# A four-batch transformer block: x of batches 2 and 3 turned into tokens by transposes, its mean taken off where the tokens are scaled

## The chip, the cores and the metric

The kernel runs on one core of a Trainium2 chip, in float32. The metric is the time of one execution in device microseconds; a kernel's time is the median of several runs. The engines are named as the profile names them: PE (TensorE), DVE (VectorE), ACT (ScalarE), POOL (GpSimd) and SP (SyncE, which only issues DMAs here).

## The reference, cut to what matters

```python
# x: (4, 96, 56, 56)
x = x + conv_attention(_ln_c(x))     # _ln_c: layer norm over the 96 channels, eps 1e-6
t = tokens(x)                        # (4, 3136, 96)
t = t + experts(_ln_t(t))            # 4 experts of width 384, the 2 best weighted by a softmax
...
def conv_attention(x):
    value = dwconv3x3(x); query = dwconv3x3(x)
    key = dwconv3x3(x, stride=2); off = dwconv3x3(x, stride=2)
    pos = tanh(offsets(gelu(norm(off))) + ref)       # (28, 28) positions
    v = bilinear_sample(value, pos)
    out = (query^T key * scale) v                    # per head, 12 heads
    return w_out @ out
```

The change concerns `_ln_c` of batches 2 and 3: `(x - mean) / sqrt(var + eps)`, with mean and variance over the channels of each pixel.

## The kernel before, in words

The five engines each run one list of instructions, written out by hand, and meet at semaphores. The four batches go through the same stages. The expert part of a batch is cut into 84 chunks of 448 tokens x 128 hidden units: three matmuls (L762 to L764), a Gelu on ACT (L1006) and a second product (L746). These chunks fill PE while DVE works on the convolutions of the next batch. How many chunks PE has issued, and how many Gelus ACT has done, before each step of the other work is given by the tables `CHUNKS_AHEAD` (PE) and `GELUS_AHEAD` (ACT), by step and position; chunk numbers run through all batches. The last 84 chunks are done alone at the end, with more exact second products.

In `rest(b)` for batch b (1 to 3) the order around the change is, on each engine:

- PE: values to tokens (L621), then `x_to_tokens(b + 1)`: x of the next batch, channels on partitions, is turned into tokens in 7 slots of 4 pieces of 112 pixels (L529), two slots between chunks; then keys (L566), chunks, then `quarters_back(b + 1)`, the "pad" blocks: 6 blocks, 3 of the upper and 3 of the lower rows, which turn the normed tokens back into channels with a halo row (L534, L551, L556). Then `key_values` (L632), `mixes`, `attended` (L662, L650).
- ACT: empties each slot of tokens into `xT` (L839), each pad block into `xpad` (L858); in `scaled` it multiplies the tokens of tiles 6, 5 and 4 by `rstd` (L831, four activations to a tile, each on 96 channels).
- DVE: `norm_x`: `bn_stats` of the tokens (L1082), `statistics` (L1059 to L1072, on 112 x 28 numbers, with three Newton steps for `rstd`), then `scale_x`, which multiplies tiles 0 to 3 by `rstd` (L1098), then `sample` (L1335, L1338).

The matmul of L529 has the matrix `ident_gate` = I - 1/96 as its moving operand, so the tokens come out with the mean already off:

```python
last = nc.tensor.matmul(bank[0:TP, j * C:(j + 1) * C], x_of(b)[:, t0:t0 + TP], ident_gate[:, 0:C], start=True, stop=True)
```

A float32 matmul stands in the trace as two records (two passes), a transpose as one. DVE signals `x_stats` when `rstd` is done; ACT's `scaled` waits for it, and the pads wait for `x_normed` (DVE's tiles) and `x_normed_act` (ACT's). PE and ACT share two PSUM banks, `pa0` and `pa1`, for the slots, the pads and some more: block n may be written when block n - 2 has been emptied. In batches 2 and 3 the tables have PE begin the pads after 69 and 145 chunks, and ACT scale its tiles at `xn=(67, 69, 69)` and `xn=(143, 144, 145)` Gelus.

POOL gathers the sampled values by indirect DMA (L1469) and adds the experts' outputs to x (L1480); DVE forms these outputs (`ye`, L1416) at points of its own list.

Of the kernel before, what the change touches and what calls it, by code (L numbers as in the profile page):

```python
# [18 lines left out]
BATCH, C, H, W = 4, 96, 56, 56  # L19
# [5 lines left out]
QUARTERS = HC // CH_PER_HEAD  # L25
QPIX = PIX // QUARTERS
SCALE = HC ** -0.5
EXPERTS, HID = 4, 4 * C
LN1_EPS, OFF_EPS, LN2_EPS = 1e-6, 1e-5, 1e-5

TP = 112
# [59 lines left out]
def dve_jobs():  # L91

    order = jobs(0, "offs", 1)
    for b in range(BATCH):
        order += jobs(b, "kv", QUARTERS) + jobs(b, "y", NY) + jobs(b, "x1c", NG)
        if b + 1 < BATCH:
# [35 lines left out]

GELUS_AHEAD = [
    dict(x1n=(0, 0, 0), x1c=(0, 0, 0, 0, 3, 3, 4), exp=(0,), gateT=(3,), offT=(10, 10), offc=(16, 17), tanh=(19,)),
    dict(valT=(42, 42, 43, 43, 44, 44, 45), xT=(45, 46, 46, 47, 47, 48, 48), keyT=(49, 49), xn=(67, 69, 69),
         pad=(69, 70, 70, 71, 71, 72), mix=(73, 73, 74, 74), x1T=(74, 74, 74, 74, 74, 74, 75), offT=(75, 76),
         x1n=(78, 80, 82), x1c=(80, 81, 83, 84, 86, 86, 87), exp=(81,), gateT=(86,), offc=(93, 94), tanh=(95,)),
    dict(valT=(118, 118, 119, 119, 120, 120, 121), xT=(121, 122, 122, 123, 123, 124, 124), keyT=(125, 125),
         xn=(143, 144, 145), pad=(145, 146, 146, 147, 147, 148), mix=(151, 151, 152, 152),
         x1T=(152, 152, 152, 152, 152, 152, 153), offT=(153, 154), x1n=(156, 158, 160),  # L140
         x1c=(158, 159, 161, 162, 164, 164, 165), exp=(159,), gateT=(164,), offc=(172, 173), tanh=(175,)),
    dict(valT=(198, 198, 199, 199, 200, 200, 201), keyT=(204, 204), mix=(233, 233, 234, 234),
# [45 lines left out]
def build(nc, t, out):  # L188
# [4 lines left out]
    with ExitStack() as ctx:  # L193
# [302 lines left out]
        def _(pe):  # L496
# [17 lines left out]
            def x_to_tokens(b, before=lambda g: None, slots=range(QT)):  # L514

                for s in slots:
                    before(s)
                    if s == 0:
                        pe.wait_ge(centred, 1)
                        if not first(b):  # L520
                            pe.wait_ge(x_in[b], 16)
                    if first(b):
                        for n, (start, end) in enumerate(X_PARTS):
                            if s == start:
                                pe.wait_ge(x_part[n], 16)
                    bank = act_bank(b, "xT", s)
                    for j in range(QUARTERS):
                        t0 = (j * QT + s) * TP
                        last = nc.tensor.matmul(bank[0:TP, j * C:(j + 1) * C], x_of(b)[:, t0:t0 + TP], ident_gate[:, 0:C], start=True, stop=True)  # L529
                    last.then_inc(act_full, 1)  # L530

            def halo(bank, at, pieces, rows):
# [3 lines left out]
            def quarters_back(b, before=lambda g: None):  # L536

                for g in range(2 * BLOCKS):
                    before(g)
                    i, low = g % BLOCKS, g // BLOCKS  # L540
                    if g == 0:
                        pe.wait_ge(x_normed, 2 * b + 1)
                        pe.wait_ge(x_normed_act, 3 * b + 1)
                    elif g == BLOCKS:
                        pe.wait_ge(x_normed, 2 * b + 2)
                        pe.wait_ge(x_normed_act, 3 * b + 3)
                    bank = act_bank(b, "pad", g)
                    if low:
                        for k in range(TOP_TILES, QT):
                            at = (k - TOP_TILES) * TP  # L550
                            nc.tensor.transpose(bank[:, at:at + TP], stationary(tiles_of(k), i), ident[0:TP, 0:TP])  # L551
                        halo(bank, LOW_PIX - W, stationary(first_tiles[:, :, 1:, :], i), 0).then_inc(act_full, 1)
                    else:
                        halo(bank, 0, stationary(last_tiles[:, :, 0:QUARTERS, :], i), 1)
                        for k in range(TOP_TILES):
                            last = nc.tensor.transpose(bank[:, W + k * TP:W + (k + 1) * TP], stationary(tiles_of(k), i), ident[0:TP, 0:TP])  # L556
                        last.then_inc(act_full, 1)
# [260 lines left out]
        def _(act):  # L818
# [22 lines left out]

            def scaled(b, before=lambda n: None):

                for n, s in enumerate(reversed(range(TOP_TILES + 1, QT))):
                    before(n)
                    act.wait_ge(x_stats, b + 1)
                    scale(x_stats_of(b), [(s * QUARTERS + j, tiles_of(s)[:, :, j, :]) for j in range(QUARTERS)]).then_inc(x_normed_act, 1)

            def padded(b, before=lambda g: None):
                for g in range(2 * BLOCKS):  # L850
# [178 lines left out]
        def _(dve):  # L1029
# [52 lines left out]
                    last = v.bn_stats(m.st[0:TP, k, :], tile(k))  # L1082
                return last

            def norm_tokens(m, b, last, eps, stats, turn):

                link(last)
                statistics(m, TP, NT, eps, False, turn).then_inc(stats, 1)
                dve.wait_ge(stats, b + 1)

            def bn_x(b, g):
                return bn(x_stats_of(b), b, g, lambda n: tiles_of(n // QUARTERS)[:, :, n % QUARTERS, :], "xT")

            def scale_x(b):
                by = x_stats_of(b).rstd[0:TP, :].rearrange("p (s o j u) -> p s o j u", j=QUARTERS, o=1, u=1)
                for s in range(TOP_TILES + 1):
                    part = tiles_of(s)
                    ins = v.tensor_tensor(part, part, by[:, s, :, :, :].to_broadcast([TP, BLOCKS, QUARTERS, CB]), ALU.mult)  # L1098
                    if s >= TOP_TILES - 1:
                        ins.then_inc(x_normed, 1)  # L1100

            def norm_x(b, turn):

                for g in range(NG):
                    last = bn_x(b, g)
                    turn()
                norm_tokens(x_stats_of(b), b, last, LN1_EPS, x_stats, turn)
                scale_x(b)
                turn()

# [427 lines left out]
```

## Time and profile before

| | |
|---|---|
| Timed runs | 748.95, 750.81, 751.0 us; median 750.81 us |
| Profiled execution, span from first to last instruction | 749.4 us |
| Busy of the span | PE 94%, PEld 66%, DVE 78%, ACT 51%, POOL 29% |
| Chain that ended last | PE 56%, DVE 19%, DMA 7%, ACT 6%, POOL 5%, issue 5% |
| Mean granted clock of TensorE | 0.985 |

The profiled execution has no time of its own in the list beside its span. Busy time is counted from the first to the last cycle of an instruction; matmuls overlap, so a busy PE can still be one that is held up. The chain is followed back from the last instruction to what released it, so it names what each stage waited for. In a timeline a row is a run of like instructions: its start, its length, and in brackets how long the engine had stood before and who released it.

### The profile page before, as it was taken

The page shows a single profiled execution, that of the slowest core. Times are in us where ns is not written, and L with a number is a line of the kernel's source. Part 1 is how long each engine was busy: PE and PEld are TensorE (multiplying, and loading weights), DVE is VectorE, ACT ScalarE, POOL GpSimd, SP SyncE. Part 2 cuts the span into 40 slices and gives each one's busy share as a digit, 9 for nine tenths or more (in the row PEclk, how much of TensorE's full clock was granted, in tenths as well). Part 3 has the DMA queues.
Part 4 walks back from the last instruction along what each step waited for, and adds up shares of the span by engine and source line. Part 5 has one row for each costly group of instructions (what it writes and reads, how often), then busy time and mean ns, then how long its engine had stood idle before and what let it go on. Part 6 is the DMA issues. An engine that isn't in the chain of part 4 may idle for free.

```text
span 749.4 us, 9619 instructions
## 1 busy us (share of the span) xinstructions
PE 707.8 (94%) x3186; PEld 495.8 (66%) x3186; DVE 582.8 (78%) x1511; ACT 384.5 (51%) x722; POOL 216.9 (29%) x184
## 2 busy tenths in 40 slices
PE   5798999799999999999999999999998999999996
PEld 5556566566676666556767566666664665788884
DVE  4889648899999858699999477899975275677774
ACT  2314124744464614744556218545542256899995
POOL 4001700012128610111168201222285121344443
PEclk9998999799999999999999999999999999999999
DMA  8007200044464530345654422435645201121111
GB/s 195 9 0 198 53 9 1 7 98 86 89 185 115 98 56 10 68 103 119 155 129 83 86 48 46 82 80 101 190 102 109 35 20 49 47 69 51 66 47 37
DMA packets 29697, 58.66 MB, mean 78 GB/s; under 512 B 6224, under 2 KB 20176, under 8 KB 29360
## 3 DMA queue, kind: packets, MB, share of 16 engines
q0 software_dynamic: 11584, 17.90, 15.4%
q1 hardware_dynamic: 14336, 32.59, 14.7%
q10 hardware_dynamic: 3728, 7.55, 3.3%
q8 instruction: 26, 0.43, 0.2%
q14 instruction: 23, 0.19, 0.1%
HBM read 30.30 MB, written 14.65 MB: 60 GB/s over the span
## 4 chain that ended last, share of the span: by engine, by line
PE 56%; DVE 19%; DMA 7%; ACT 6%; POOL 5%; issue 5%; POOLq 0%; ACTq 0%
PE py L746 9%; PE pd L662 8%; PE ph L578 7%; DVE val L1133 6%; POOL big L1469 4%; DMA xbuf<-ye 4%; DVE query L1133 3%; PE pa L650 3%; PE pa L529 2%; PE ph L762 2%; PE ph L782 2%; PE ph L784 2%; PE ph L763 2%; PE ph L783 2%; PE ph L764 2%
## 5 line engine op out<-in xcount | busy, mean ns | idle before, releaser
L746 PE MATMUL py<-hid,w 128*96 128x448 f32 x504 | 234.4, 546 | 11.5 <-ACT hid L1006 8.7
L1006 ACT ACTIVATE hid<-ph,b 128x448 f32<-128x448 f32 x252 | 158.9, 632 | 148.1 <-PE ph L764 144.8
L762 PE MATMUL ph<-x_hi,w_hi 96*128 96x448 f32 x252 | 164.4, 653 | 0.0
L1480 POOL DMA_DIRECT2D xbuf<-ye x76 | 66.6, 877 | 327.2 <-DMA xbuf<-ye 163.2
L1469 POOL DMA_INDIRECT big<-value_table,rows x64 | 87.8, 1372 | 90.5 <-DVE rows L1193 56.5
L746 PEld LDWEIGHTS py<-hid,w 128*96 128x96 f32 x504 | 81.6, 165 | 31.2 <-ACT hid L1006 12.6
L763 PE MATMUL ph<-x_lo,w_hi 96*128 96x448 f32 x252 | 93.5, 371 | 0.0
L764 PE MATMUL ph<-x_hi,w_lo 96*128 96x448 f32 x252 | 92.8, 368 | 0.0
L1482 POOL TENSOR_TENSOR xbuf<-xbuf,ye 96x448 f32<-96x448 f32 x36 | 53.9, 1497 | 102.6 <-DVE ye L1416 99.9
L1416 DVE SCALAR_TENSOR_TENSOR ye<-py,b,gate_all 96x448 f32<-96x448 f32 x112 | 75.3, 674 | 9.3 <-PE py L746 7.3
L1443 DVE TENSOR_TENSOR hid_lo<-hid,hid_hi 128x448 fp32r<-128x448 f32 x84 | 59.7, 710 | 27.3 <-ACT hid L1015 27.1
L1133 DVE SCALAR_TENSOR_TENSOR query<-xpad,conv_w,query 128x784 f32<-128x784 f32 x80 | 78.3, 1027 | 0.5
L1133 DVE SCALAR_TENSOR_TENSOR val<-xpad,conv_w,val 128x784 f32<-128x784 f32 x80 | 78.3, 1026 | 0.4
L762 PEld LDWEIGHTS ph<-x_hi,w_hi 96*128 96x128 f32 x252 | 48.3, 192 | 41.1 <-issue 39.7
L763 PEld LDWEIGHTS ph<-x_lo,w_hi 96*128 96x128 f32 x252 | 48.8, 194 | 35.6 <-issue 35.0
L662 PE MATMUL pd<-query,mix_area 128*96 128x392 f32 x192 | 67.2, 493 | 0.0
L1015 ACT ACTIVATE hid_hi<-ph,b 128x448 fp32r<-128x448 f32 x84 | 53.3, 634 | 6.9 <-PE ph L784 1.7
L1015 ACT ACTIVATE hid<-ph,b 128x448 f32<-128x448 f32 x84 | 52.5, 625 | 0.0
L826 ACT ACTIVATE big<-pa 112x400 f32<-112x400 f32 x28 | 14.0, 502 | 70.6 <-PE pa L650 70.6
L764 PEld LDWEIGHTS ph<-x_hi,w_lo 96*128 96x128 f32 x252 | 47.9, 190 | 3.3
L662 PEld LDWEIGHTS pd<-query,mix_area 128*96 128x96 f32 x192 | 29.6, 164 | 23.9 <-issue 23.9
L1354 DVE TENSOR_TENSOR xbuf<-pd,xbuf 96x392 f32<-96x392 f32 x32 | 17.9, 560 | 32.8 <-PE pd L662 32.5
(165 smaller groups left out, 1081.2 us busy)
## 6 DMA issues: line engine op xcount, KB each, us to landing
gate_all<-gate_rows SPq DMA_DIRECT2D x56, 336.0 KB, 3.5
xbuf<-ye POOLq DMA_DIRECT2D x76, 168.0 KB, 3.4
value_table<-valT ACTq DMA_DIRECT2D x6, 1176.0 KB, 8.9
out<-xbuf SPq DMA_DIRECT2D x28, 168.0 KB, 2.0
xbuf<-in_x SPq DMA_DIRECT2D x3, 1176.0 KB, 10.1
value_table<-valT SPq DMA_DIRECT2D x2, 672.0 KB, 5.3
big<-value_table,rows POOLq DMA_INDIRECT x64, 2.8
value_table<-valT SPq DMA_DIRECT2D x2, 504.0 KB, 5.0
```

The source lines that it names most:

```text
L662: last = nc.tensor.matmul(bank[0:C, 0:YPIX], mix[:, q, i, :], query[:, i, h * YPIX:(h + 1) * YPIX], start=(i == 0), stop=(i == BLOCKS - 1))
L746: nc.tensor.matmul(py[e % 2][0:C, 0:GPIX], w2[:, c, :], hid[:, k % 3, :], start=(j == 0), stop=(j == CPE - 1)).then_inc(hid_used, 1)
L762: nc.tensor.matmul(bank, w1_hi[:, cols], xh(b, g), start=True, stop=False)
L763: nc.tensor.matmul(bank, w1_hi[:, cols], xl(b, g), start=False, stop=False)
L764: nc.tensor.matmul(bank, w1_lo[:, cols], xh(b, g), start=False, stop=True).then_inc(hid_full, 1)
L1006: nc.scalar.activation(hid[:, k % 3, :], ph[k % 2][:, 0:GPIX], ACT.Gelu, bias=b1[:, k % NCH:k % NCH + 1]).then_inc(hid_act, 1)
L1015: nc.scalar.activation(dst[:, k % 3, :], ph[k % 2][:, 0:GPIX], ACT.Gelu, bias=b1[:, k % NCH:k % NCH + 1]).then_inc(ready, 1)
L1133: ins = v.scalar_tensor_tensor(to, src, w, to, ALU.mult, ALU.add)
L1416: v.scalar_tensor_tensor(ye[0:C, e, :], py[e % 2][0:C, 0:GPIX], b2[:, e:e + 1], gate_all[0:C, e, :], ALU.add, ALU.mult).then_inc(ye_ready, 1)
L1443: v.tensor_tensor(hid_lo[:, m % 2, :], hid[:, k % 3, :], hid_hi[:, k % 3, :].bitcast(f32), ALU.subtract).then_inc(hid_lo_ready, 1)
L1469: p.indirect_dma_start(got[:, tile, r, :, :].rearrange("p a c -> p (a c)"), None, table, bass.IndirectOffsetOnAxis(ap=rows[:, r, tile:tile ...
L1480: pool.dma_start(to, ye[0:C, e, :], accum_op=ALU.add).then_inc(ye_summed, 16)
```

## The change

For batches 2 and 3 (`SHIFTED_FROM = 2`) the 28 matmuls by `ident_gate` become 28 transposes with `ident`, so the tokens keep their mean. `statistics` now also makes the mean, and one more operation turns it into -mean * rstd. ScalarE and VectorE then scale with `x * rstd + (-mean * rstd)`: ScalarE with Identity, scale and bias per partition, over tiles 6, 5, 4 and now also 3; VectorE with a tensor_scalar for each of 4 quarters of tiles 0, 1 and 2. VectorE adds to `x_normed` twice at its end, and the counts that PE waits for take the fourth tile in. The table gives ScalarE a fourth point.

```diff
-    dict(... xn=(67, 69, 69),
+    dict(... xn=(67, 68, 69, 69),
...
-         xn=(143, 144, 145), pad=(145, 146, 146, 147, 147, 148), ...
+         xn=(142, 143, 144, 145), pad=(145, 146, 146, 147, 147, 148), ...
...
                     for j in range(QUARTERS):
                         t0 = (j * QT + s) * TP
-                        last = nc.tensor.matmul(bank[0:TP, j * C:(j + 1) * C], x_of(b)[:, t0:t0 + TP], ident_gate[:, 0:C], start=True, stop=True)
+                        if b < SHIFTED_FROM:
+                            last = nc.tensor.matmul(bank[0:TP, j * C:(j + 1) * C], x_of(b)[:, t0:t0 + TP], ident_gate[:, 0:C], start=True, stop=True)
+                        else:
+                            last = nc.tensor.transpose(bank[0:TP, j * C:(j + 1) * C], x_of(b)[:, t0:t0 + TP], ident[0:C, 0:C])
                     last.then_inc(act_full, 1)
...
-                        pe.wait_ge(x_normed_act, 3 * b + 1)
+                        pe.wait_ge(x_normed_act, 3 * b + 1 + max(0, b - SHIFTED_FROM))
...
-                        pe.wait_ge(x_normed_act, 3 * b + 3)
+                        pe.wait_ge(x_normed_act, 3 * b + 3 + max(0, b + 1 - SHIFTED_FROM))
...
             def scaled(b, before=lambda n: None):
 
-                for n, s in enumerate(reversed(range(TOP_TILES + 1, QT))):
+                m = x_stats_of(b)
+                for n, s in enumerate(reversed(range(TOP_TILES + (0 if b >= SHIFTED_FROM else 1), QT))):
                     before(n)
                     act.wait_ge(x_stats, b + 1)
-                    scale(x_stats_of(b), [(s * QUARTERS + j, tiles_of(s)[:, :, j, :]) for j in range(QUARTERS)]).then_inc(x_normed_act, 1)
+                    if b < SHIFTED_FROM:
+                        scale(m, [(s * QUARTERS + j, tiles_of(s)[:, :, j, :]) for j in range(QUARTERS)]).then_inc(x_normed_act, 1)
+                        continue
+                    for j in range(QUARTERS):
+                        k, tile = s * QUARTERS + j, tiles_of(s)[:, :, j, :]
+                        last = nc.scalar.activation(tile, tile, ACT.Identity, scale=m.rstd[0:TP, k:k + 1], bias=m.mean[0:TP, k:k + 1])
+                    last.then_inc(x_normed_act, 1)
...
-            def norm_tokens(m, b, last, eps, stats, turn):
+            def norm_tokens(m, b, last, eps, stats, turn, shifted=False):
 
                 link(last)
-                statistics(m, TP, NT, eps, False, turn).then_inc(stats, 1)
+                ins = statistics(m, TP, NT, eps, shifted, turn)
+                if shifted:
+                    link(ins)
+                    ins = v.scalar_tensor_tensor(m.mean[0:TP, :], m.mean[0:TP, :], -1.0, m.rstd[0:TP, :], ALU.mult, ALU.mult)
+                ins.then_inc(stats, 1)
                 dve.wait_ge(stats, b + 1)
...
             def scale_x(b):
+                if b >= SHIFTED_FROM:
+                    for s in range(TOP_TILES):
+                        for j in range(QUARTERS):
+                            k, tile = s * QUARTERS + j, tiles_of(s)[:, :, j, :]
+                            ins = v.tensor_scalar(tile, tile, rstd[0:TP, k:k + 1], mean[0:TP, k:k + 1], ALU.mult, ALU.add)
+                    ins.then_inc(x_normed, 2)
+                    return
```

How ScalarE's list stands around batch 2's tiles, in `rest(1)`. `hid` is a chunk's Gelu, `xT` a token tile, `xpad` the emptying of a pad block. Before:

```order
L1006 ACTIVATE hid<-ph,b 128x448 x18
L831 ACTIVATE xT<-xT,rstd 112x3x32 x4
L1006 ACTIVATE hid<-ph,b 128x448 x2
L831 ACTIVATE xT<-xT,rstd 112x3x32 x8
L858 ACTIVATE xpad<-pa 128x7x56
L1006 ACTIVATE hid<-ph,b 128x448
L858 ACTIVATE xpad<-pa 128x7x56 x2
L1006 ACTIVATE hid<-ph,b 128x448
```

Now:

```order
L1017 ACTIVATE hid<-ph,b 128x448 x18
L857 ACTIVATE xT<-xT,mean,rstd 112x3x32 x4
L1017 ACTIVATE hid<-ph,b 128x448
L857 ACTIVATE xT<-xT,mean,rstd 112x3x32 x4
L1017 ACTIVATE hid<-ph,b 128x448
L857 ACTIVATE xT<-xT,mean,rstd 112x3x32 x8
L869 ACTIVATE xpad<-pa 128x7x56
L1017 ACTIVATE hid<-ph,b 128x448
L869 ACTIVATE xpad<-pa 128x7x56 x2
L1017 ACTIVATE hid<-ph,b 128x448
```

Each scaling reads `mean` too, a Gelu stands between the first two tiles, and there are 16 activations instead of 12 ahead of the first `xpad`.

The same list around batch 3's tiles, in `rest(2)`. Before:

```order
L1006 ACTIVATE hid<-ph,b 128x448 x18
L831 ACTIVATE xT<-xT,rstd 112x3x32 x4
L1006 ACTIVATE hid<-ph,b 128x448
L831 ACTIVATE xT<-xT,rstd 112x3x32 x4
L1006 ACTIVATE hid<-ph,b 128x448
L831 ACTIVATE xT<-xT,rstd 112x3x32 x4
L858 ACTIVATE xpad<-pa 128x7x56
L1006 ACTIVATE hid<-ph,b 128x448
```

Now:

```order
L1017 ACTIVATE hid<-ph,b 128x448 x17
L857 ACTIVATE xT<-xT,mean,rstd 112x3x32 x4
L1017 ACTIVATE hid<-ph,b 128x448
L857 ACTIVATE xT<-xT,mean,rstd 112x3x32 x4
L1017 ACTIVATE hid<-ph,b 128x448
L857 ACTIVATE xT<-xT,mean,rstd 112x3x32 x4
L1017 ACTIVATE hid<-ph,b 128x448
L857 ACTIVATE xT<-xT,mean,rstd 112x3x32 x4
L869 ACTIVATE xpad<-pa 128x7x56
L1017 ACTIVATE hid<-ph,b 128x448
```

The first tile now comes one Gelu earlier, after 17 of them in a row instead of 18, and a fourth tile stands ahead of the first `xpad`.

VectorE's list at the end of batch 2's statistics, in `rest(1)`: `rstd` is the last Newton step, `ye` an expert output, `key_area` the first sampling. Before:

```order
L1070 SCALAR_TENSOR_TENSOR su<-sv,rstd 112x28
L1071 TENSOR_TENSOR su<-su,rstd 112x28
L1072 SCALAR_TENSOR_TENSOR rstd<-su,rstd 112x28
L1098 TENSOR_TENSOR xT<-xT,rstd 112x3x128
L1098 TENSOR_TENSOR xT<-xT,rstd 112x384 x3
L1416 SCALAR_TENSOR_TENSOR ye<-py,b,gate_all 96x448
L1335 TENSOR_SCALAR key_area<-big,w 98x96 x2
```

Now:

```order
L1081 SCALAR_TENSOR_TENSOR su<-sv,rstd 112x28
L1082 TENSOR_TENSOR su<-su,rstd 112x28
L1083 SCALAR_TENSOR_TENSOR rstd<-su,rstd 112x28
L1102 SCALAR_TENSOR_TENSOR mean<-mean,rstd 112x28
L1114 TENSOR_SCALAR xT<-xT,rstd,mean 112x3x32 x12
L1438 SCALAR_TENSOR_TENSOR ye<-py,b,gate_all 96x448
L1357 TENSOR_SCALAR key_area<-big,w 98x96 x2
```

Four scalings of a whole tile have become twelve of a quarter of one, and -mean * rstd is made ahead of them.

## Rows read from the trace of the kernel before

**Rows 1.** The page: busy time by engine, and the chain that ended last by engine.

```profile
PE 707.8 (94%) x3186; PEld 495.8 (66%) x3186; DVE 582.8 (78%) x1511; ACT 384.5 (51%) x722; POOL 216.9 (29%) x184
...
PE 56%; DVE 19%; DMA 7%; ACT 6%; POOL 5%; issue 5%; POOLq 0%; ACTq 0%
```

**Rows 2.** The chain in order of time (start us, us, what): TensorE's turning steps.

```profile
66.45 3.14 PE pa L529 x16
...
94.68 3.98 PE pa L529 x40
...
519.88 0.66 PE pa L621 x6
```

**Rows 3.** The same chain, 244 to 250 us: statistics of batch 2's x.

```profile
244.15 0.11 DVE sd L1059
...
247.28 0.20 DVE su L1071
...
247.50 0.20 DVE rstd L1072
...
249.46 0.99 PE py L746 x2
```

**Rows 4.** Timeline of ScalarE, 247 to 253 us (start us, us, engine, line, operation, [idle before]).

```profile
247.72 1.17 ACT L831 ACTIVATE xT<-xT,rstd 112x96 f32<-112x96 f32 x4 [0.43 <-DVE rstd L1072]
...
252.04 0.48 ACT L858 ACTIVATE xpad<-pa 128x392 f32<-128x392 f32 x1
```

**Rows 5.** Timeline of TensorE, 252 to 258 us: batch 2's third pad, batch 1's keys.

```profile
252.61 0.39 PE L534 MATMUL pa<-ident,xT 112*128 112x56 f32 x2
...
257.64 2.78 PE L632 MATMUL pd<-keyT,key_area 98*96 98x384 f32 x8
```

**Rows 6.** Timeline of VectorE, 247 to 259 us.

```profile
247.72 1.97 DVE L1098 TENSOR_TENSOR xT<-xT,rstd 112x384 f32<-112x384 f32 x4
...
258.58 0.27 DVE L1335 TENSOR_SCALAR key_area<-big,w 98x96 f32<-98x96 f32 x1 [2.29 <-DMA big<-value_table,rows]
```

**Rows 7.** Lines of ScalarE by form: line, shapes, count | busy us, mean ns.

```profile
L831 ACT ACTIVATE xT<-xT,rstd 112x96 f32<-112x96 f32 x36 | 10.2, 363 | 4.6 <-DVE rstd L1072 4.6
...
L858 ACT ACTIVATE xpad<-pa 128x392 f32<-128x392 f32 x12 | 5.7, 492 | 1.9 <-PE pa L556 1.8
...
L881 ACT ACTIVATE mix_area<-pa,ln_gb 96x392 f32<-96x392 f32 x8 | 5.3, 671 | 1.7 <-PE pa L511 1.7
...
L893 ACT ACTIVATE val<-ph,conv_b 128x392 f32<-128x392 f32 x4 | 2.3, 587 | 23.7 <-PE ph L578 23.7
```

**Rows 8.** Timeline of VectorE, 164 us: scaling by two per-partition operands.

```profile
164.27 2.00 DVE L1165 TENSOR_SCALAR kv_area<-kv_area,mean,rstd 98x96 f32<-98x96 f32 x8
```

**Rows 9.** Timelines of VectorE, ScalarE and TensorE, 402 to 421 us: batch 3's x.

```profile
402.49 0.19 DVE L1072 SCALAR_TENSOR_TENSOR rstd<-su,rstd 112x28 f32<-112x28 f32 x1
...
402.93 1.16 ACT L831 ACTIVATE xT<-xT,rstd 112x96 f32<-112x96 f32 x4
...
407.15 0.48 ACT L858 ACTIVATE xpad<-pa 128x392 f32<-128x392 f32 x1
...
408.00 0.33 PE L534 MATMUL pa<-ident,xT 112*128 112x56 f32 x2
...
412.96 2.78 PE L632 MATMUL pd<-keyT,key_area 98*96 98x384 f32 x8
...
415.29 0.27 DVE L1335 TENSOR_SCALAR key_area<-big,w 98x96 f32<-98x96 f32 x1 [3.86 <-DMA big<-value_table,rows]
...
420.89 2.79 PE L632 MATMUL pd<-keyT,key_area 98*96 98x384 f32 x8 [1.06 <-DVE kv_area L1348]
```

**Rows 10.** Busy time in windows: engines' busy us (instructions), granted clock, DMA share, GB/s.

```profile
64.00:66.00 2.00, 2.00 (x16) 2.00 (x14) 1.93 (x6) 0.49 (x1) 0.00 (x0) 0.51 0.85 279
...
303.00:306.00 3.00, 1.38 (x6) 0.60 (x5) 2.49 (x11) 2.97 (x8) 0.00 (x0) 1.00 0.02 4
```

**Rows 11.** Timeline of TensorE, 62 us.

```profile
62.26 1.80 PE L621 MATMUL pa<-ident,val 128*112 128x128 f32 x9 [1.81 <-ACT mix_area L881]
```

More of the change, by code:

```diff
@@ L27 @@
 SCALE = HC ** -0.5
+SHIFTED_FROM = 2
 EXPERTS, HID = 4, 4 * C
@@ L134 @@
     dict(x1n=(0, 0, 0), x1c=(0, 0, 0, 0, 3, 3, 4), exp=(0,), gateT=(3,), offT=(10, 10), offc=(16, 17), tanh=(19,)),
-    dict(valT=(42, 42, 43, 43, 44, 44, 45), xT=(45, 46, 46, 47, 47, 48, 48), keyT=(49, 49), xn=(67, 69, 69),
+    dict(valT=(42, 42, 43, 43, 44, 44, 45), xT=(45, 46, 46, 47, 47, 48, 48), keyT=(49, 49), xn=(67, 68, 69, 69),
          pad=(69, 70, 70, 71, 71, 72), mix=(73, 73, 74, 74), x1T=(74, 74, 74, 74, 74, 74, 75), offT=(75, 76),
@@ L138 @@
     dict(valT=(118, 118, 119, 119, 120, 120, 121), xT=(121, 122, 122, 123, 123, 124, 124), keyT=(125, 125),
-         xn=(143, 144, 145), pad=(145, 146, 146, 147, 147, 148), mix=(151, 151, 152, 152),
+         xn=(142, 143, 144, 145), pad=(145, 146, 146, 147, 147, 148), mix=(151, 151, 152, 152),
          x1T=(152, 152, 152, 152, 152, 152, 153), offT=(153, 154), x1n=(156, 158, 160),
@@ L1106, in norm_x @@
                     turn()
-                norm_tokens(x_stats_of(b), b, last, LN1_EPS, x_stats, turn)
+                norm_tokens(x_stats_of(b), b, last, LN1_EPS, x_stats, turn, shifted=b >= SHIFTED_FROM)
                 scale_x(b)
```

## Prediction

> **What bounds the kernel now.** I read the page's busy table and its summary of the chain first, then the chain piece by piece, then the timelines of TensorE, ScalarE and VectorE where batches 2 and 3 of x are brought in. The busy table and the chain's summary [rows 1] show TensorE busy 94% and 56% of the chain, so every matmul looks worth saving. The chain in order of time says otherwise for this stage: between 211 and 248 us it runs through VectorE, whose queue (taps, statistics of x) has no idle time there, and it ends at the last Newton step of `rstd` at 247.50 + 0.20 = 247.70 [rows 3]. ScalarE, which had stood 0.43 us for it, then scales its first tile [rows 4], and TensorE's next second product comes at 249.46 [rows 3]. TensorE is filled with expert chunks meanwhile, but their number ahead of the "pad" blocks is fixed by a table: time that it saves earlier is time that it waits there.
>
> **The change, part by part.**
>
> *TensorE.* 28 matmuls by `ident_gate` become 28 transposes in each of two batches. In the chain 20 such matmuls (40 records) took 3.98 us at the full clock, 0.199 us each, and 6 transposes of 128 columns 0.66 us, 0.110 each [rows 2]. So 28 x 0.089 = 2.5 us less per batch, 5.0 in all. I cost this gain at nothing: it falls at 211 to 222 us, and what ends the stage is `rstd`, which doesn't move with it. TensorE reaches the pads' last chunk 2.5 us earlier and stands. On the trace there is no cover that turns it into time, since the chunks are handed out by count.
>
> On that point the Trainium skill (Perfetto Trace Analysis, section Transposes) says that a logical transpose should be a transpose and not a standard matmul. The rows agree on the price of one; by that rule alone the kernel would be 5.0 us faster, and this is the first rival below.
>
> *VectorE, statistics.* Three operations of 112 x 28 are added ahead of the semaphore: two that only issue, like the one that takes 0.11 in the chain, and one that waits for the last Newton step, a linked step of 247.50 - 247.28 = 0.22 [rows 3]. `x_stats` comes 0.44 us later.
>
> *VectorE, scaling.* Four tensor_tensors of 384 elements take 1.97 us [rows 6]. Twelve tensor_scalars of 96 elements with two pointer operands take their place; the nearest row has eight of 98 x 96 in 2.00 us [rows 8], 0.25 each, 3.0 us for twelve. VectorE is then 0.44 + 1.03 = 1.5 us later, and behind it stand the samplings. These are covered: VectorE waits 2.29 us for a gather at 258.58 [rows 6], and longer a batch later [rows 9]. Without that cover it would cost these 1.5 us. Both `x_normed` counts now come with the last operation, at 247.70 + 0.44 + 3.0 = 251.1; the first pad asks after the stalled second product at about 251.2, so this is not the last wait.
>
> *ScalarE, scaling.* This is the term that counts. Before: 12 activations in a batch, 0.363 us each [rows 7]; four in a row took 1.17 us [rows 4], so each starts (1.17 - 0.363) / 3 = 0.269 after the one before. Now 16, as Identity with scale and bias both read per partition. The trace has no such operation. Lower bound: as the Copy with a scale, 0.269. Nearest rows for the bias: Identity with a bias on 392 columns 0.587 against Copy 0.492 [rows 7], 0.095 more, so 0.364 a step. Upper bound: Gelu with scale and bias 0.671 against that Copy [rows 7], 0.179 more, so 0.448. I take 0.364, because the scale is already in the 0.269 and the bias alone is added: 16 x 0.364 - 12 x 0.269 = 5.82 - 3.23 = +2.6 us.
>
> *Who waits for it.* ScalarE is in order. It scales the first two tiles, each with a Gelu behind it, then the other tiles, and only then empties pad block 0. TensorE owns two banks for the pads, so its third block waits for that emptying, and everything behind it (keys with values, mixes, the whole of `attended`) follows in order.
>
> - Batch 2 (during batch 1): ScalarE starts emptying block 0 at 252.04 [rows 4] and TensorE starts the third block at 252.61 [rows 5], 0.09 after it ends. Now 252.04 + 0.44 + 2.6 = 255.1, and TensorE's block at 255.6: +3.0 us. Its key products, which started at 257.64 without a wait [rows 5], start at 260.6. The last sample waits for a gather until 258.58 [rows 6] and takes some 1.5 us more, until 260.1, ahead of that: no slack is left to take the 3.0 up.
> - Batch 3 (during batch 2): emptying began at 407.15; `rstd` was done at 402.49 + 0.19 = 402.68, and ScalarE started its tiles at 402.93, 0.25 late [rows 9]. Now it stands waiting, so that lag goes; the table lets it scale one Gelu earlier, so three Gelus and not two lie between the tiles: one is (252.04 - 247.72 - 12 x 0.269) / 2 = 0.54 [rows 4]. 407.15 + 0.44 - 0.25 + 2.6 + 0.54 = 410.5, and TensorE's third block moves from 408.00 to 411.0, +3.0. Its key products at 412.96 go to 416.0, but the later two quarters had waited 1.06 us for VectorE and the gathers at 420.89 [rows 9]; that much is absorbed: +1.9.
>
> After each place TensorE is fully busy through `attended`, VectorE gets its next work from it, and POOL's sums and gathers follow VectorE, so I see no place that takes the delay up. Sum: +3.0 + 1.9 = **+4.9 us**. Made against the profiled execution: 749.4 + 4.9 = 754.3 of span. The median of the timed runs, 750.81, stands 1.4 above that span; with that added, **755.7 us**. With the lower bound of the activation (0.269) only 4 x 0.269 = 1.1 is added in place of 2.6: about +1.4 and +0.35, which gives 752.6 (in the second place TensorE came 408.00 - 407.63 = 0.37 us after the emptying before [rows 9], and that is taken off too). With the upper bound (0.448) 3.9 is added: +4.3 and +3.2, which gives 758.3.
>
> About 0.3% of the time, 2.25 us, is what a measurement can tell from no change.
>
> **The rivals.**
>
> 1. *Faster: TensorE's gain is kept.* Place: the pads of batches 2 and 3. If TensorE were what the pads wait for, each batch would be 2.5 us shorter, 750.8 - 5.0 = 745.8. For it: the 94% and 56% [rows 1]. Against it: ScalarE already waits for `rstd` before [rows 4]. It decides from the point where `rstd` would be ready 2.5 us or more ahead of its present time, and nothing in the change moves it ahead.
>
> 2. *No change that can be told: a wait takes most of the delay up.* If the operations cost their lower bound, or if the gathers of batches 2 and 3 start as early as before, because POOL and the DMA queue set them and not the late batch before, then one of the two delays disappears: between 750.8 + 1.75 = 752.6 and 750.8 + 1.9 = 752.7. For it: VectorE waits for gathers in both batches [rows 6, 9]. Against: those gathers need values and offsets that come after `attended`.
>
> 3. *Slower still: the clock.* TensorE would stand for the 2.5 us of gain and the 0.44 + 4 x 0.095 = 0.8 by which the first Gelu behind a tile is later, over 3 us, at 247 to 250, and about 4 at 401 to 405. The trace shows 1.62 us without work (3.00 - 1.38) leave the granted clock at 1.00, its level of 2.4 GHz [rows 10]. It also shows it at 0.51, the level of 1.2 GHz, at 64 us [rows 10], after TensorE had stood 1.81 us and done transposes [rows 11]; there a matmul takes 3.14 / 8 = 0.39 us [rows 2]. The new stops lie between, and transposes of the pads follow them. Price: from the stop to the third pad TensorE had 252.61 - 249.46 = 3.15 us of work [rows 3, 5]. Taken twice, less some 2 us in which it would have waited for ScalarE anyway, that is +1.2 in one batch; with nothing taken off in the other, +3.15 more: 757 to 760.
> The Trainium skill (TensorE: Matmul & The Clock Gate, Part 4: PE-mode transpose) says that transposes don't count as activity for the full clock; the row at 64 us agrees, and by that rule this case becomes likelier, 757 to 760.
>
> 4. *The transposes are no cheaper than the matmuls.* Then TensorE stands 2.5 us less in each batch, and the end is the same 755.7, since the tiles on ScalarE decide; it has no chance of its own.
>
> **How the numbers follow.** Forecast (ScalarE's longer tiles are the new last wait, 752.6 to 758.3): 0.66. Rival 1: 0.05. Rival 2: 0.14. Rival 3: 0.15. The predicted time is the forecast's, 755.7. The range goes from the lower bound, 752.6, to 759.0, which takes in the upper bound of the activation and most of the clock case; left out are rival 1, a part of rival 2 and the tail of rival 3. Faster by over 0.3%: 0.05 (rival 1). Within 0.3%: 0.14 (rival 2). Slower: 0.81.
>
> **What would show it.** In the changed kernel's profile: L533's transposes at about 0.11 us where L529 had 0.199; `x_stats` 0.44 us after its old place; ScalarE's 16 tiles as Identity with a step of about 0.36; a wait of TensorE of over 3 us for a Gelu at the end of the chunks before the pads, and one of some 2 us for the emptying of pad block 0; the key products of batch 1 at about 260.6. The forecast is wrong if the third pad of batch 2 starts before 253.5, or if the key products of batch 2 come no later against their gathers than before. The clock case shows as a granted clock near 0.5 right after 250 or 405 us.

## The result and the profile after

Median 757.67 us (756.0, 757.39, 757.95, 758.04) against 750.9 of the kernel before beside it: ratio 1.0086, 95% interval 1.0063 to 1.0108, slower by 6.8 us by the medians and by 6.5 by the ratio. Repeated later, it took 757.67 again, ratio 1.0077 (1.0049 to 1.0104). The forecast was 755.7, range 752.6 to 759.0. The profiled execution took 756.0 us, span 754.2, mean granted clock 0.976 against 0.985 before.

The page after: PE has 56 records less, DVE 22 more, ACT 8 more. In the chain PE has grown and DVE shrunk [rows 1]. The second products stand longer for their Gelus: 11.5 us of idle time ahead of them before, 8.7 of it for Gelus, and 18.9 now, 13.1 of it for Gelus. Their row before, then the page now:

```profile
L746 PE MATMUL py<-hid,w 128*96 128x448 f32 x504 | 234.4, 546 | 11.5 <-ACT hid L1006 8.7
```

```profile
PE 705.8 (94%) x3130; PEld 489.6 (65%) x3130; DVE 585.6 (78%) x1533; ACT 388.6 (52%) x730; POOL 215.8 (29%) x184
...
PE 65%; DVE 14%; ACT 7%; DMA 5%; issue 3%; POOL 3%; POOLq 0%; ACTq 0%
...
L750 PE MATMUL py<-hid,w 128*96 128x448 f32 x504 | 235.4, 548 | 18.9 <-ACT hid L1017 13.1
```

The timeline of TensorE around batch 2's x. The turning starts at 209.31, against 210.96 before: this execution is 1.65 us early from stages ahead of the change (in the repetition only 0.2), so every shift below is counted from the start of the turning.

```profile
209.31 0.50 PE L533 MATMUL pa<-ident,xbuf 96*112 96x96 f32 x4
...
213.28 0.82 PE L533 MATMUL pa<-ident,xbuf 96*112 96x96 f32 x8
...
223.71 0.96 PE L750 MATMUL py<-hid,w 128*96 128x448 f32 x2 [0.78 <-ACT hid L1017]
...
233.53 0.96 PE L750 MATMUL py<-hid,w 128*96 128x448 f32 x2 [1.43 <-DVE ye L1438]
...
248.31 0.99 PE L750 MATMUL py<-hid,w 128*96 128x448 f32 x2 [0.94 <-ACT hid L1017]
...
253.51 0.43 PE L538 MATMUL pa<-ident,xT 112*128 112x56 f32 x2 [1.51 <-ACT xpad L869]
...
258.58 2.78 PE L636 MATMUL pd<-keyT,key_area 98*96 98x384 f32 x8
```

The turning takes 2.94 us less than before (217.40 - 209.31 against 221.99 - 210.96, from its start to the row of L570 behind it, L566 before). Three waits use that up, 0.78, 1.43 and 0.94 us, and a fourth of 1.51, for ScalarE's emptying of pad block 0, ends the stage. None of the four stood there before; the third pad of [rows 5] has no bracket. VectorE and ScalarE in the same place:

```profile
245.98 0.19 DVE L1102 SCALAR_TENSOR_TENSOR mean<-mean,rstd 112x28 f32<-112x28 f32 x1
246.20 3.16 DVE L1114 TENSOR_SCALAR xT<-xT,rstd,mean 112x96 f32<-112x96 f32 x12
...
257.88 0.27 DVE L1357 TENSOR_SCALAR key_area<-big,w 98x96 f32<-98x96 f32 x1 [2.06 <-DMA big<-value_table,rows]
```

```profile
246.20 1.54 ACT L857 ACTIVATE xT<-xT,mean,rstd 112x96 f32<-112x96 f32 x4 [0.88 <-DVE mean L1102]
...
250.11 2.97 ACT L857 ACTIVATE xT<-xT,mean,rstd 112x96 f32<-112x96 f32 x8
252.97 0.48 ACT L869 ACTIVATE xpad<-pa 128x392 f32<-128x392 f32 x1
```

From ScalarE's first tile to the emptying of pad block 0 it is 252.97 - 246.20 = 6.77 us, before 252.04 - 247.72 = 4.32 [rows 4]: +2.45. Counted from the start of the turning, the emptying, the third pad and the keys all stand 2.55 to 2.59 later (keys: 258.58 + 1.65 - 257.64).

Batch 3, ScalarE first, then TensorE. All of it is 0.93 later on arrival (367.6 against 366.7 for the first turning).

```profile
404.23 1.54 ACT L857 ACTIVATE xT<-xT,mean,rstd 112x96 f32<-112x96 f32 x4 [3.25 <-DVE mean L1102]
...
411.52 0.49 ACT L869 ACTIVATE xpad<-pa 128x392 f32<-128x392 f32 x1
```

```profile
406.34 1.01 PE L750 MATMUL py<-hid,w 128*96 128x448 f32 x2 [3.31 <-ACT hid L1017]
...
408.30 1.81 PE L750 MATMUL py<-hid,w 128*96 128x448 f32 x2
...
412.56 0.32 PE L538 MATMUL pa<-ident,xT 112*128 112x56 f32 x2
...
417.52 2.78 PE L636 MATMUL pd<-keyT,key_area 98*96 98x384 f32 x8
```

Emptying: 411.52 - 0.93 - 407.15 = +3.44; keys: 417.52 - 0.93 - 412.96 = +3.63 [rows 9]. `attended` behind them starts 2.36 later (430.82 - 0.93 - 427.53), so 1.27 us are absorbed on the way. After the stop of 3.31 us two second products took 1.81 us, not 1.0. The windows (length, busy of PE, PEld, DVE, ACT, POOL, granted clock, DMA share, GB/s) show why:

```profile
406.00:407.00 1.00, 0.66 (x3) 0.43 (x3) 1.00 (x5) 1.00 (x4) 0.70 (x2) 1.00 0.25 75
407.00:408.00 1.00, 1.00 (x4) 0.64 (x2) 1.00 (x4) 1.00 (x4) 0.88 (x1) 0.59 0.96 115
408.00:409.00 1.00, 1.00 (x3) 0.40 (x2) 1.00 (x6) 1.00 (x4) 0.82 (x1) 0.50 0.59 126
409.00:410.00 1.00, 1.00 (x4) 0.43 (x3) 1.00 (x6) 1.00 (x3) 0.69 (x2) 0.50 0.35 68
410.00:411.00 1.00, 1.00 (x10) 1.00 (x9) 1.00 (x6) 1.00 (x4) 0.69 (x2) 0.70 0.57 191
```

The granted clock fell to its lower level: 0.41 + 0.50 + 0.50 + 0.30 = 1.71 us of work at the full clock lost, though here ScalarE was late anyway: its emptying ends at 412.01, and the third pad starts 0.55 after that.

A second such stretch stands at 581 to 585, in the last stage with keys, and there nothing hides it. First the rows before, where the clock stayed at 1.00, then the rows and one window now:

```profile
577.15 0.96 PE L746 MATMUL py<-hid,w 128*96 128x448 f32 x2 [1.88 <-DVE ye L1416]
577.95 2.75 PE L632 MATMUL pd<-keyT,key_area 98*96 98x384 f32 x8
```

```profile
580.25 0.96 PE L750 MATMUL py<-hid,w 128*96 128x448 f32 x2 [1.89 <-DVE ye L1438]
581.05 4.44 PE L636 MATMUL pd<-keyT,key_area 98*96 98x384 f32 x8
```

```profile
582.00:583.00 1.00, 1.00 (x3) 0.53 (x2) 0.56 (x1) 0.00 (x0) 0.69 (x1) 0.50 0.24 75
```

The key products take 4.44 us instead of 2.75. The delay against before grows from 3.10 us at their start (581.05 against 577.95) to 4.78 at the `attended` behind them (589.34 against 584.56), and the end is 4.8 later than before in all.

### The profile page after: what moved, and what is told of

Same layout as the page of the kernel before. It is cut to its first block, busy times and chain, and to the rows that moved or that the text cites. A ratio compares the mean times of both kernels' runs of the same rounds, so it can differ in the third digit from the quotient of the medians.

```text
span 754.2 us, 9537 instructions
## 1 busy us (share of the span) xinstructions
PE 705.8 (94%) x3130; PEld 489.6 (65%) x3130; DVE 585.6 (78%) x1533; ACT 388.6 (52%) x730; POOL 215.8 (29%) x184
## 4 chain that ended last, share of the span: by engine, by line
PE 65%; DVE 14%; ACT 7%; DMA 5%; issue 3%; POOL 3%; POOLq 0%; ACTq 0%
PE py L750 14%; PE pd L666 8%; PE ph L582 6%; PE ph L766 3%; PE ph L767 3%; PE ph L768 3%; DVE query L1155 3%; DVE val L1155 3%; DMA value_table<-valT 3%; POOL big L1491 3%; PE pa L654 3%; PE pd L636 3%; PE pa L531 2%; PE ph L786 2%; PE ph L788 2%
## 5 line engine op out<-in xcount | busy, mean ns | idle before, releaser
L750 PE MATMUL py<-hid,w 128*96 128x448 f32 x504 | 235.4, 548 | 18.9 <-ACT hid L1017 13.1
```

What stands on the lines that cost most here:

```text
L750: nc.tensor.matmul(py[e % 2][0:C, 0:GPIX], w2[:, c, :], hid[:, k % 3, :], start=(j == 0), stop=(j == CPE - 1)).then_inc(hid_used, 1)
```

## The experiments

Shifts are read from one trace of each kernel, from the start of a batch's turning to a later place, against the same places in the trace of the kernel before. "Batch 2" ends at the keys of batch 1, "batch 3" at `attended` of batch 2.

**Transposes alone, twice.** `ident_gate` to transposes for b >= 2 in the kernel before; the scaling stays, so the mean is not taken off there.

```diff
+ if b < 2: matmul(..., ident_gate[:, 0:C])
+ else:     nc.tensor.transpose(..., ident[0:C, 0:C])
```

> The kernel before with one part of the change: the 28 float32 products by ident_gate are transposes in batches 2 and 3. Everything else is as before, so the mean of each token is not taken off in those two batches, and the output differs from the reference there. My theory (TensorE's gain is worth nothing, because VectorE's rstd ends the stage): the same time as before within 1 us, with TensorE standing some 2.5 us longer ahead of the pads of each batch, third pad of batch 2 at 252 to 253 us. Rival 1 (the gain is kept): 5.0 us less than before, about 745.8. Rival 3 (the clock): a longer stop with transposes behind it lowers the granted clock, 1 to 3 us more than before.

754.37 us against 750.99, ratio 1.0046 (1.0014 to 1.0078): slower, which only rival 3 had. But in its trace the keys of both stages are right, -0.22 and -0.22, and the clock holds ahead of the pads. What it lost came between them. A sum of experts' outputs, a DMA that POOL issues, took 9.98 us to land where its neighbours took 3.3 to 5.0; POOL issued one more sum only then, and the gathers, next in its list, came 4.9 us later than before. TensorE then stood 2.15 us for VectorE ahead of the later keys of batch 1, the granted clock fell to 0.50, and 3.41 us of work were lost at 266 to 274. The chain of waits, in order of time, and the stop:

```profile
210.97 5.04 DMA xbuf<-ye
...
216.54 9.98 DMA xbuf<-ye
...
228.16 1.81 POOL big L1472
```

```profile
264.70 3.72 PE L635 MATMUL pd<-keyT,key_area 98*96 98x384 f32 x8 [2.15 <-DVE kv_area L1351]
```

So it was run again.

> The kernel before with the transposes alone, again (the mean is not taken off in batches 2 and 3), to see whether its 3.4 us over before, which my theory did not expect, come back, and whether the slow sum (9.98 us to land) ahead of the gathers of batch 1 in its trace does. If that was chance: the key products of batch 1 and batch 2 as in the kernel before within 0.5 us, sums landing in under 5.5 us, time within 1.5 us of before. If it follows from the transposes: the same sum again at 216 us and 3 us over before.

752.34 against 751.85, ratio 1.0012 (0.9989 to 1.0035), with the keys at -0.29 and -0.38 and the gathers from 224.79. By the medians the gain on TensorE is worth nothing by itself. The sum issued at 217.21 still took 7.3 us, not under 5.5 as I expected; in the kernel before, the one at 216.19 took 7.0. What was different in the first trace is that its sums were already 3.9 us behind by 198 us, ahead of the first transpose at 211.9, so that one more had to follow the slow one: that lateness does not come from the edit. Two things are not shown: why the first group's median was higher too, and whether `attended` of batch 2, which came 1.49 and 1.08 us earlier than in the trace before, did so by the transposes or because the wait of 1.06 [rows 9] is that one trace's own.

**Matmuls by the identity in the change.** The other way round.

```diff
- nc.tensor.transpose(..., ident[0:C, 0:C])
+ nc.tensor.matmul(..., ident[0:C, 0:C], start=True, stop=True)
```

> The change with its transposes undone alone: 28 float32 products by the plain identity per batch in place of the transposes, all scaling as in the change. Nothing of the computation is left out. My theory: the same time as the change, 755 to 758, since TensorE then only stands about 2.5 us less for the Gelu and pads that wait for ScalarE. Rival 1: 5 us slower than the change, 761 to 763. Rival 3: 1 to 3 us faster than the change, because the stop of 3.3 us at 403 to 406 becomes shorter and the clock stays at 1.00.

759.38 us, 1.0128 (1.0096 to 1.0161). Batch 2 +2.67, batch 3 +1.98, the same delays as in the change within 0.4; the stop ahead of batch 3's pads is 1.68 us and the clock stays up there, but rival 3's gain of 1 to 3 us does not come. It is slower than the change by 1.7 us by the medians and by 3 to 4 by the ratios, between my theory (755 to 758) and rival 1 (761 to 763), though the intervals overlap. Of the 1.4 us between its trace and that of the repeated change, 0.93 stand there already at the start of batch 2's turning (211.70 against 210.77), ahead of which the two kernels are the same. That a part of the transposes' gain is kept somewhere else is not excluded.

**ScalarE without the bias, then with 12 activations.** The bias left out:

```diff
- nc.scalar.activation(tile, tile, ACT.Identity, scale=rstd, bias=mean)
+ nc.scalar.activation(tile, tile, ACT.Copy, scale=rstd)
```

> The change with ScalarE's tiles as a Copy with the scale alone, so the bias, and with it the mean of the tokens that ScalarE scales in batches 2 and 3, is left out. My theory: the step falls from 0.363 to 0.269 us, 16 x 0.094 = 1.5 us less in each batch: the drain of pad block 0 in batch 2 ends 1.5 us earlier than in the change and in batch 3 1.5 us too, of which the later keys keep 1.1 to 1.5; 2.6 to 3.0 us faster than the change, 754.5 to 755.3, that is 3.5 to 4.5 above before. Rival 2 (something else takes the delay up): within 1 us of the change.

756.17, 1.0059 (1.0025 to 1.0093), about 1 us more than expected. Eight activations take 2.23 us (2.97 in the change); batch 2 falls from +2.59 to +1.19, by 1.40 where 1.5 was expected. Batch 3 falls only from +2.36 to +1.92. There ScalarE is ready at 410.35 and then waits for a pad block that TensorE turns at half speed after a stop of 2.92 us:

```profile
409.19 1.16 ACT L857 ACTIVATE xT<-xT,rstd 112x96 f32<-112x96 f32 x4
410.56 0.50 ACT L869 ACTIVATE xpad<-pa 128x392 f32<-128x392 f32 x1 [0.20 <-PE pa L560]
```

Tile 3 back on VectorE:

```diff
- DVE scales tiles 0 to 2 (12 operations), ACT tiles 6 to 3 (16)
+ DVE scales tiles 0 to 3 (16 operations), ACT tiles 6 to 4 (12); xn as before the change
```

> The change with tile 3 of the tokens back on VectorE, as before the change: 16 tensor_scalars there in place of 12, 12 Identity activations on ScalarE in place of 16, and the table's places for ScalarE's tiles as before. Nothing of the computation is left out. My theory: ScalarE's path gets 4 x 0.363 = 1.45 us shorter in batch 2, and 1.45 plus a Gelu of 0.5 in batch 3, while VectorE's 1.0 us more is covered by its waits for gathers: about 3 us faster than the change, 754 to 755. Rival (VectorE is what the samplings wait for): 1.0 us lost per batch against the 1.45 won, within 1 us of the change.

754.01, 1.0047 (1.0025 to 1.0068), 2 to 3 us under the change by the ratios, near the 3 expected. Batch 2 is +1.23 for +2.59: 1.36 of the 1.45 taken off. In batch 3 the emptying comes at +1.48 for +3.44, also as expected, but `attended` gains nothing in the trace (+2.68): after a stop of 1.92 us, with the pads' transposes behind a single second product, 3.4 us are lost at half speed. This trace is of the slowest of the twelve executions (759.07); what the others did there is not shown.

**Chunks handed out later.** The change was run again, and beside it three kernels with later tables: the pads and all that follows are handed out 1 chunk later from batch 2's pads on and 2 more from batch 3's (1 more in the kernel before). They are the change, the change with tile 3 on VectorE, and the kernel before. The edit for batch 2's stage, cut:

```diff
- pad=(69, 69, 70, 71, 71, 72), kv=(72, 72, 73, 73), ...
+ pad=(70, 70, 71, 72, 72, 73), kv=(73, 73, 74, 74), ...
```

> The changed kernel itself, again, beside the three other kernels of this group on the same chip. Both theories (delay by ScalarE alone; delay by ScalarE and half-speed stretches behind the new stops) expect 5 to 7 us over before. By the second, its mean granted clock over many executions lies 0.002 to 0.003 below that of before, and each 0.0023 is one stretch of 1.71 us lost.

> The change, with one expert chunk more ahead of the pads of batch 2 and two more ahead of those of batch 3 (the tables only: ScalarE's tiles, the pads and all that follows are handed out 1 and 3 chunks later). If TensorE's saved 2.5 us are idle time only because the chunks are handed out by count, chunks of 1.36 us fill the stops of 0.94 and 3.31 us and are missing later, where TensorE is the bound: 0.5 to 1 us less in batch 2, about 2.5 less in batch 3, and no half-speed stretch at 407 to 411; 3 to 4 us under the change, 1.5 to 3 over before. If something else (VectorE, the gathers) bounds the later stages, the same time as the change within 1 us.

> Both edits together: tile 3 of the tokens on VectorE and the one and two chunks more ahead of the pads. If the two costs are separate, 2.5 to 3.5 us under the kernel with tile 3 on VectorE alone, so within 1 us of before. If they are the same idle time counted twice, no more than 1 us under the better of the two.

> The kernel before, its products and scaling untouched, with one expert chunk more ahead of the pads of batches 2 and 3. TensorE has no idle time there in the kernel before, so the tiles and the pads come 1.36 us later and the chunk is missing later: the same time as before within 1 us. If it is faster by 2 us or more, the table and not the saved time of the transposes is what the other two kernels gain from.

The change again: 757.67, batch 2 +2.66, batch 3 +2.25, mean granted clock over its runs 0.9787 against 0.9815 before. The three with later tables came out far slower, as no theory had it: 782.19 (1.0395), 780.44 (1.0384) and 765.59 (1.0195). TensorE's waits for VectorE's outputs, in total, times and longest, of the change, of the change with later tables and of the kernel before with later tables:

```profile
PE py L750 <- DVE ye L1438: 5.9, 6, 1.9
```

```profile
PE py L735 <- DVE ye L1423: 30.5, 16, 5.0
```

```profile
PE py L731 <- DVE ye L1401: 13.8, 10, 2.7
```

In the kernel before this total is 2.7. So the change with later tables waits 24.6 us more, as much as the 24.5 by which its median is above the change's, and the kernel before 11.1 more of its 14.3. I had left out that VectorE forms each output (three chunks) at fixed points of its own list, and that the output's PSUM bank is wanted again two outputs later. A count of chunks is thus tied to VectorE's list for the rest of the program; these runs tell nothing of what filling the stops is worth.

**Only ScalarE's order.**

```diff
- xn=(67, 68, 69, 69)   xn=(142, 143, 144, 145)
+ xn=(68, 69, 69, 69)   xn=(144, 145, 145, 145)
```

> The change with ScalarE's order alone changed: one Gelu in batch 2 and two in batch 3 go ahead of the first scaled tile, into the 0.88 and 3.25 us that ScalarE stands for the statistics; nothing lies between the later tiles. My theory (the drain of pad block 0 is the last wait): 0.2 us less in batch 2; in batch 3 two Gelus of 0.51 off the path, drain at -1.0 us, TensorE's stop of 3.31 us falls to some 1 us, and the granted clock stays at 1.00 at 405 to 415: 1.2 to 2 us under the change. If the stop itself is what costs (the clock rival), more than that, 2 to 3 us under the change; if VectorE or the gathers decide, the same time as the change.

757.46, 1.0079 (1.0050 to 1.0108): the same as the change, where 1.2 to 2 us less were expected. Batch 2 +2.45, batch 3 +2.67. ScalarE empties block 0 at 410.44, 1.2 us earlier counted from the start of the turning, as meant, but TensorE, which now waits for VectorE's tiles, stands 2.04 us right ahead of the pads' transposes, and the clock falls again (3.4 us lost at 407 to 415). In this trace the clock took what ScalarE won.

**Pad block 0 emptied early.** Tile 3 on VectorE, Gelus first, and the first emptying ahead of tile 4, which only the fourth pad reads.

```diff
- scaled(all three tiles); padded(blocks 0 to 5)
+ scaled(tiles 6, 5); padded(block 0); scaled(tile 4); padded(blocks 1 to 5)
```

> The change repaired: tile 3 on VectorE, the Gelus ahead of ScalarE's first tile as in the run beside this, and pad block 0 emptied after ScalarE's second tile and not after all, since tile 4 is first read by the fourth pad block. The end of VectorE's first twelve tensor_scalars then sets the first pad: statistics + 0.44 + 3.1 us against the 2.6 to 3.0 of before, so +0.7 to +1.0 us in each batch: 1.5 to 2 us over before, about 5 under the change. If ScalarE's drain were not what holds TensorE, no less than the kernel with tile 3 on VectorE alone.

755.44, 1.0044 (1.0014 to 1.0074): 3.3 to 3.6 us over before, where 1.5 to 2 were expected. Batch 2 +0.93, as worked out. Batch 3 +2.79 for +0.7 to 1.0: its first pad still starts at +0.77, its keys at +4.06. Between them lie a stop of 2.21 us, transposes and half speed. TensorE and its clock:

```profile
407.25 0.67 PE L538 MATMUL pa<-ident,xT 112*128 112x56 f32 x2 [2.21 <-DVE xT L1117]
407.72 0.78 PE L560 MATMUL pa<-ident,xT 112*128 112x112 f32 x3
...
410.35 1.70 PE L750 MATMUL py<-hid,w 128*96 128x448 f32 x2
```

```profile
408.00:409.00 1.00, 1.00 (x7) 1.00 (x6) 1.00 (x4) 0.41 (x2) 0.95 (x1) 0.50 0.51 106
...
412.00:413.00 1.00, 1.00 (x7) 1.00 (x6) 1.00 (x6) 0.04 (x1) 0.59 (x1) 0.50 0.58 183
```

**The stop filled.** Against the run above, one chunk is moved within the stage, from between the pads to ahead of them, with the output that it needs.

```diff
- pad=(69, 69, 70, 71, 71, 72)    pad=(145, 145, 146, 147, 147, 148)
+ pad=(70, 70, 70, 71, 71, 72)    pad=(146, 146, 146, 147, 147, 148)
- xn=(68, 68, 69)    xn=(144, 144, 145)
+ xn=(68, 69, 70)    xn=(144, 145, 146)
- OUTPUTS_AHEAD[2]: ..., 46, 46, 47, ...
+ OUTPUTS_AHEAD[2]: ..., 46, 47, 47, ...
```

> The repaired change (pad block 0 emptied early) with TensorE's stops filled: the expert chunk that stood between the second and third pad block goes ahead of the first in batches 2 and 3, ScalarE's Gelu for it between its first two tiles, and in batch 3 VectorE's output that this chunk's bank needs goes ahead of the scaling (0.6 us). All else as in the run with the early emptying; no chunk moves out of the stage. My theory by now: the stop of 2.2 us ahead of the transposes of batch 3 lets the granted clock fall, and the two stretches at half speed (3.4 us lost) are what held that run at +2.8 us in batch 3. Filled, the clock stays at 1.00 at 405 to 415: batch 2 at -0.3 to 0 us against before, batch 3 at 0 to +0.6: within 1.5 us of before. If the clock falls regardless of the stop, or the later waits take it back, 3 us or more over before.

754.79 against 752.16, 1.0028 (1.0005 to 1.0052): the lowest ratio of the versions with the change's scaling, though the intervals of the run above and of the one with tile 3 on VectorE overlap it, and more than the 1.5 us over before that were expected. The same places:

```profile
406.00 0.99 PE L750 MATMUL py<-hid,w 128*96 128x448 f32 x2 [1.05 <-ACT hid L1020]
407.11 0.43 PE L538 MATMUL pa<-ident,xT 112*128 112x56 f32 x2
407.38 0.47 PE L560 MATMUL pa<-ident,xT 112*128 112x112 f32 x3
```

```profile
408.00:409.00 1.00, 0.83 (x10) 0.62 (x8) 1.00 (x5) 1.00 (x3) 0.70 (x2) 1.00 0.20 50
...
412.00:413.00 1.00, 1.00 (x7) 0.84 (x6) 1.00 (x5) 0.91 (x3) 0.00 (x0) 1.00 0.78 127
```

The stop is 1.05, the clock stays at 1.00, and batch 3 is at -0.25: 3.0 us better than the run above in the trace. The order of the work changed too, but the place of the gain is the clock's: from the first pad to the keys the run above fell back by 3.3 us, with 3.4 lost to the clock, and this one by none (+1.34, then +1.02). Batch 2 misses: its keys come at +0.45, but `attended` at +1.36, since the later keys now wait 0.70 for VectorE, which waits 2.10 for a gather as before [rows 6], but for one that lands 2.1 later (259.40 + 1.27 against 258.58). What holds that gather was not tried. The delay at the end of this trace comes from a third place:

```profile
577.23 0.96 PE L750 MATMUL py<-hid,w 128*96 128x448 f32 x2 [1.94 <-DVE ye L1442]
578.03 4.44 PE L636 MATMUL pd<-keyT,key_area 98*96 98x384 f32 x8
```

At these keys the execution is 0.08 us behind the kernel before (578.03 against 577.95); behind a stop of 1.94 the clock falls at 578 to 582, as in the change, and `attended` starts 1.77 later (586.33 against 584.56). The end is 1.8 later. No version beat the kernel before.

## Why the prediction was right, step by step

- *TensorE's gain costed at nothing*: right by the runs of the transposes alone (1.0012 repeated; keys at -0.2 to -0.4 us), with the doubt that the medians of the matmuls in the change leave. L533 takes 0.82 / 8 = 0.10 us, and the gain in batch 2 is 2.94 us, not 2.5. I expected one wait of over 3 us ahead of the pads; in batch 2 it is spread, and one part of it is for VectorE's outputs; in batch 3 it is the 3.31.
- *Statistics, +0.44*: ScalarE's first tile came +0.13 in batch 2 and 404.23 - 0.93 - 402.93 = +0.37 in batch 3, where +0.19 was forecast.
- *ScalarE's step, 0.364*: the mean activation is 0.459 us, 0.363 + 0.096; eight take 2.97, a step of 0.36. The bias on all 16 costs 1.40 us in batch 2, the four more activations 1.36. The two runs share the bias of those four, some 4 x 0.095 = 0.38, so together they come to 2.4, near the +2.45 from the first tile to the emptying; the forecast had 2.6.
- *Who waits for it*: right in batch 2, +2.6 for the forecast's +3.0 (the statistics were over-priced by 0.3), and in the emptying of batch 3 (+3.44 for +3.35). The third pad of batch 2, at 253.51, is near my bound of 253.5 only because this execution is 1.65 early.
- *Batch 3, +1.9*: +2.36 (+2.25 repeated). The third pad was forecast at +3.0 and came at +3.63, behind ScalarE and the clock; the gathers then took up 1.27, not 1.06. The sum of both places is 2.6 + 2.4 = 5.0 for 4.9.
- *The median, 2.0 above the forecast*: most likely the clock, a term that I left out. I held it for a rival with 757 to 760, instead of a part of the forecast. Its stops were really there (3.31, forecast about 4), it fell in batch 3 and not in batch 2, and it was mostly hidden behind ScalarE in the change itself. In the repeated runs the mean granted clock is 0.003 lower than before, some 2 us of 755, and in the change's own trace the delay grows by 1.7 us behind the stop at 580 us, a place I had not looked at. That each run loses there is not shown. Behind stops of 1.84 to 2.32 us in that stage the clock fell in five of six traces with the change's scaling, and in none of three without it (1.87 to 1.97), later tables left aside; why is open.
- *The range* held by luck in part. Its upper end was there for a dearer activation (0.448 a step) and for the clock, and the activation measured 0.36: the forecast's own terms give 755.7, and what lies above that is not among them.
- *Rivals*: 1 is refuted for these places by the transposes alone and by the matmuls in the change. 2 holds for a part: 1.27 us absorbed in batch 3, none in batch 2. 3 was right that the clock falls, and had the place in batch 3, but in the change's trace what it cost in the open came in the last stage with keys. 4 is out: the transposes are cheaper.

## What to carry to other kernels

A cheaper operation is worth what the stage's last wait allows; look which engine that is, and whether the edit that pays for it (here a bias on 16 activations and a mean on 12 more DVE operations) lands on that engine. Time saved on TensorE and left idle can cost: behind stops of 1.92 to 3.31 us ahead of batch 3's pads the clock fell, and taking ScalarE's delay away then gained little or nothing in that stage of the traces until the stop was filled. Where work is handed out by count, a chunk can be moved within a stage; moved across stages it ran into another engine's list and cost 14 to 25 us.

## What the runs showed of the hardware

- Ahead of batch 3's pads the granted clock fell to 0.50 behind stops of TensorE of 1.92, 2.04, 2.21, 2.92, 3.15 and 3.31 us, and held behind 1.05 and 1.68; in batch 2 it held behind 1.34, 1.36 and 1.51. In the last stage with keys (577 to 585 us) it fell behind 1.86, 1.89, 1.94, 2.02 and 2.32 and held behind 1.84, 1.87, 1.88 and 1.97. On each fall the trace shows 1.7 or 3.4 us of work lost.
- The length of the stop alone does not decide it. In the kernel before, the clock held behind 1.62 [rows 10] and fell behind 1.80 at 623 us, with a chunk's matmuls next; in the run with pad block 0 emptied early it fell behind 1.62 at 304 us.
- The Trainium skill (TensorE: Matmul & The Clock Gate, Part 4: PE-mode transpose) says that transposes don't count as activity for the full clock in the same way. Ahead of batch 3's pads the traces agree so far as this: with transposes right behind the stop, or behind one second product, 3.4 us were lost (stops of 1.92 to 2.21), with a whole chunk's matmuls first 1.7 (stops of 2.92 to 3.31). But transposes are not needed for it: in the first run of the transposes alone 3.4 us were lost at 266 to 274 with key products behind a stop of 2.15.
- A DMA that adds to a tile takes 3.4 to 3.6 us to land in the median of twelve of the traces at 160 to 360 us, and up to 10.0 there. Issued near 216 us, with the DMA engines' share at 1.0, it took 7.0 in the kernel before, 7.3 and 7.6 in two other traces, and 9.98 in the first of the transposes alone. POOL issues in the order of its list: in that trace the late sum made the gathers behind it late.
